# A graph-attention layer with residual and layernorm on one core: three edits in the prologue

## The reference, cut to what matters

```
dep_emb = dep_emb_table[adj]                                   # 64 wide
hi_t = h @ W1_w[:384] + dep_emb @ W1_w[384:] + W1_b
hj_t = h @ W2_w[:384] + dep_emb @ W2_w[384:] + W2_b
relevance = sum(hi_t * hj_t, axis=-1)                          # 64 x 64 for each graph
A = softmax(where(adj != 0, relevance, -1e9))
h_syn = relu((A @ h) @ gcn_w + gcn_b)
out = layernorm(x + h_syn @ Wo_w + Wo_b)
```

## Time and profile before

| | before |
|---|---|
| median of 3 runs | 372.6 us (372.27 to 373.13) |
| the profiled execution | 373.2 us |
| its span, first to last instruction | 371.3 us |
| PE busy | 364.5 us, 98% of the span |
| DVE busy | 274.7 us, 74% |
| ACT busy | 181.5 us, 49% |
| POOL busy | 145.1 us, 39% |
| PE's share of the chain that ended last | 95% |

### The profile page before, as it was taken

How to read it: one execution, slowest core, us unless ns; L and a number is a source line. 1 busy time by engine, 2 the same in 40 slices (tenths; PEclk the granted TensorE clock), 3 DMA queues, 4 the chain that set the end, 5 groups by cost and what they waited for, 6 DMA issues and landing times.

```text
span 371.3 us, 9946 instructions
## 1 busy us (share of the span) xinstructions
PE 364.5 (98%) x3827; PEld 316.8 (85%) x3827; DVE 274.7 (74%) x776; ACT 181.5 (49%) x374; POOL 145.1 (39%) x108
## 2 busy tenths in 40 slices
PE   8999999999999999999999999999999999999994
PEld 5688898988889898888989889898988989898894
DVE  1579778687786868788686777858677786877956
ACT  1576717164372715527272561816347181625574
POOL 1513551716134171513517152261714327141814
PEclk9999999999999999999999999999999999999998
DMA  7996014464443556354365524435553444550033
GB/s 221 352 327 200 24 29 170 158 187 156 139 145 96 173 169 184 116 158 162 89 182 169 179 94 155 160 118 184 169 160 108 129 159 149 171 171 4 2 127 132
DMA packets 43412, 55.48 MB, mean 149 GB/s; under 512 B 10368, under 2 KB 37632, under 8 KB 43392
## 3 DMA queue, kind: packets, MB, share of 16 engines
q1 hardware_dynamic: 42592, 54.44, 46.3%
q10 hardware_dynamic: 800, 0.77, 0.6%
HBM read 42.61 MB, written 12.58 MB: 149 GB/s over the span
## 4 chain that ended last, share of the span: by engine, by line
PE 95%; DMA 2%; DVE 1%; SPq 1%; ACT 0%; issue 0%; POOL 0%
PE banks L471 28%; PE banks L473 27%; PE banks L472 27%; PE banks L531 7%; PE banks L497 7%; DMA xt_sb<-in_x_t_dram 2%; DVE m_lo L920 0%; SPq L398 0%; ACT xt_hi L749 0%; PE banks L616 0%; DVE stats L871 0%; DVE xt_sb L866 0%; SPq L394 0%; POOL rstd L1239 0%; ACT xt_sb L832 0%
## 5 line engine op out<-in xcount | busy, mean ns | idle before, releaser
L1171 POOL TENSOR_TENSOR y_sb<-y_sb,wob_sb 128x1536 f32<-128x1536 f32 x15 | 52.8, 3522 | 88.0 <-DVE y_sb L888 73.9
L783 ACT CAST z_hi<-banks 128x512 fp32r<-128x512 f32 x48 | 26.6, 588 | 96.6 <-PE banks L531 90.8
L866 DVE TENSOR_TENSOR y_sb<-banks,y_sb 128x384 f32<-128x384 f32 x60 | 33.4, 556 | 47.3 <-PE banks L473 43.7
L472 PE MATMUL banks<-wo_lo,hs_hi 128*128 128x384 f32 x180 | 60.5, 336 | 0.0
L471 PE MATMUL banks<-wo_hi,hs_hi 128*128 128x384 f32 x180 | 60.5, 336 | 0.0
L473 PE MATMUL banks<-wo_hi,hs_lo 128*128 128x384 f32 x180 | 60.5, 336 | 0.0
L471 PE MATMUL banks<-z_hi,gcn_hi 128*128 128x512 f32 x144 | 58.3, 405 | 0.0
L471 PE MATMUL banks<-xt_hi,m_hi 128*128 128x512 f32 x144 | 57.1, 397 | 0.5 <-DVE u_sb L922 0.5
L473 PE MATMUL banks<-xt_hi,m_lo 128*128 128x512 f32 x144 | 56.5, 392 | 0.0
L473 PE MATMUL banks<-z_hi,gcn_lo 128*128 128x512 f32 x144 | 56.5, 392 | 0.0
L472 PE MATMUL banks<-z_lo,gcn_hi 128*128 128x512 f32 x144 | 56.1, 390 | 0.0
(11 more groups left out here) (108 smaller groups left out, 614.7 us busy)
## 6 DMA issues: line engine op xcount, KB each, us to landing
x_sb<-in_x_dram SPq DMA_DIRECT2D x16, 768.0 KB, 4.7
xt_sb<-in_x_t_dram SPq DMA_DIRECT2D x15, 768.0 KB, 6.4
y_sb<-in_x_dram SPq DMA_DIRECT2D x15, 768.0 KB, 4.5
out_dram<-y_sb SPq DMA_DIRECT2D x30, 384.0 KB, 2.5
adj_sb<-in_adj_dram SPq DMA_DIRECT2D x32, 64.0 KB, 3.0
xt_sb<-in_x_t_dram SPq DMA_DIRECT2D x2, 384.0 KB, 7.1
xt_sb<-in_x_dram SPq DMA_DIRECT2D x1, 768.0 KB, 6.2
w2t_sb<-in_w_t_dram SPq DMA_DIRECT2D x3, 192.0 KB, 4.6
```

The lines of the kernel that those rows point to most:

```text
L472: pe.matmul(acc, a_hi, b_lo, start=False, stop=False)
L783: act.copy(by_graph(z_hi[:, f, :]), mixed(f)).then_inc(zhi, 1)
L866: dve.tensor_tensor(y_home(g, slot)[:, q, :], out_bank(g, q)[:, 0:HID], y_home(g, slot)[:, q, :], ALU.add).then_inc(added, 1)
L1171: pool.tensor_tensor(y_home(g, slot), y_home(g, slot), wob_sb[:].rearrange("p (o n) -> p o n", o=1).to_broadcast([P, PAIRS, HID]), ALU.add ...
```

## The change

Four edits, all in the prologue.

- The c products and the waits ahead of them move from behind M's first round to between its second and third blocks.
- The u product, one plain fp32 product of `ones` and `u_diag`, becomes two fp32r products of `ones_r` (a rounded copy of `ones`) with `u_hi` and `u_lo`. VectorE makes `ones_r` by one more copy, `u_hi` by the three instructions that made `u_diag`, and `u_lo` by three more, each of which reads `ident` and `u_hi` and takes a column of `u_sb` as scalar.
- Rounding the second half of group 0's x^T moves from ScalarE (L749) to VectorE, between the low parts of the first half and those of M. GpSimd's low part of it waits for a new semaphore `xt0_half`.
- GpSimd's later `split_x` counts one fewer in `xhi`, since ScalarE no longer adds one for that half. VectorE also waits once for its own `ones`.

```diff
@@ TensorE
-            def m_stage(c):
+            def m_stage(c, blocks=range(C)):
                 pe.wait_ge(w12_loaded[c], 32)
-                for d in range(C):
+                for d in blocks:
...
             pe.wait_ge(zero_column, 1)
-            m_stage(0)
+            m_stage(0, range(C - 1))
...
             mm.then_inc(c_mm, 1)
+            m_stage(0, range(C - 1, C))
             pe.wait_ge(c2_ready, 2)
...
             pe.wait_ge(u_diag_ready, 1)
-            pe.matmul(U_BANK[:, 0:HID], ones[:].to_broadcast([P, P]), u_diag, start=True, stop=True).then_inc(u_mm, 1)
+            pe.matmul(U_BANK[:, 0:HID], ones_r[:].to_broadcast([P, P]), u_hi[:], start=True, stop=False)
+            pe.matmul(U_BANK[:, 0:HID], ones_r[:].to_broadcast([P, P]), u_lo[:], start=False, stop=True).then_inc(u_mm, 1)
@@ ScalarE
-            act.wait_ge(xt_loaded[0], 16)
-            act.copy(xt_hi[:, 0, :, GT // 2:GT], xt_sb[:, 0, :, GT // 2:GT]).then_inc(xhi, 1)
@@ VectorE
+            dve.wait_ge(xt_loaded[0], 16)
+            dve.tensor_copy(xt_hi[:, 0, :, GT // 2:GT], xt_sb[:, 0, :, GT // 2:GT]).then_inc(xt0_half, 1)
             for d in range(C):
                 dve.wait_ge(m_hi_ready, d + 1)
...
             dve.wait_ge(u_sb_ready, 1)
+            dve.tensor_copy(ones_r[:], ones[:])
             for d in range(C):
-                a = dve.tensor_scalar(u_diag[:, d * P:(d + 1) * P], ident[:], u_sb[:, d:d + 1], None, ALU.mult)
+                a = dve.tensor_scalar(u_hi[:, d * P:(d + 1) * P], ident[:], u_sb[:, d:d + 1], None, ALU.mult)
+            a.then_inc(u_hi_ready, 1)
+            dve.wait_ge(u_hi_ready, 1)
+            for d in range(C):
+                a = dve.scalar_tensor_tensor(u_lo[:, d * P:(d + 1) * P], ident[:], u_sb[:, d:d + 1],
+                                             f32(u_hi[:, d * P:(d + 1) * P]), ALU.mult, ALU.subtract)
             a.then_inc(u_diag_ready, 1)
@@ GpSimd
             def split_x(g, slot):
-                pool.wait_ge(xhi, g + 1)
+                pool.wait_ge(xhi, g)
...
-            pool.wait_ge(xhi, 1)
+            pool.wait_ge(xt0_half, 1)
             pool.tensor_tensor(xt_lo[:, 0, :, GT // 2:GT], xt_sb[:, 0, :, GT // 2:GT],
                                f32(xt_hi[:, 0, :, GT // 2:GT]), ALU.subtract).then_inc(xlo, 1)
```

More of the change, by code:

```diff
@@ L155, in gnn_layernorm_kernel @@
         ones = sb("ones", [P, 1])
+        ones_r = sb("ones_r", [P, 1], F32R)
         zero = sb("zero", [P, 1])
@@ L169, in gnn_layernorm_kernel @@
         u_sb = sb("u_sb", [P, C])
-        u_diag = onehot[:].rearrange("p m t -> p (m t)")[:, PAIRS * HID:(PAIRS + 1) * HID]
+        u_hi = sb("u_hi", [P, HID], F32R)
+        u_lo = sb("u_lo", [P, HID], F32R)
         products = onehot[:].rearrange("p m t -> p (m t)")[:, 0:PAIRS * HID].rearrange("p (q d) -> p q d", d=HID)
@@ L227, in gnn_layernorm_kernel @@
         xt0_hi = sem("xt0_hi")
+        xt0_half = sem("xt0_half")
         xt0_lo = sem("xt0_lo")
@@ L238, in gnn_layernorm_kernel @@
         u_sb_ready = sem("u_sb_ready")
+        u_hi_ready = sem("u_hi_ready")
         u_diag_ready = sem("u_diag_ready")
@@ L895, in _ @@
             dve.memset(ones[:], 1.0).then_inc(ones_ready, 1)
+            dve.wait_ge(ones_ready, 1)
             dve.memset(adj_max[:], 0).then_inc(max_zero, 1)
```

## The result

| | before | after |
|---|---|---|
| median | 372.75 us (4 runs) | 376.89 us (4 runs, 376.77 to 377.16) |
| profiled execution | 373.2 us | 376.88 us |
| its span | 371.3 us | 375.1 us |
| ratio | | 1.0107, 95% interval 1.0093 to 1.012 |

A forecast was written before the change was run, and what follows sets the result against it. TensorE's own list, once through the prologue, was taken to bound the kernel. A u product starting 2.48 us later, +0.07 after a pause, -0.32 for cheaper products, gave +2.2 on the 372.6 us median: 374.8 us, range 372.0 to 375.6.

The forecast's parts named there:

- want the same port at the same time: Prologue: GpSimd asks at 14.97 and gets the SBUF port before VectorE's third `u_lo`, due at 15.13.
- 2.7 us of standing still: Ahead of the u product: TensorE idle from about 16.2 to 18.9 us, waiting for `u_lo`.
- `u_lo` at 0.85 us for three: VectorE, prologue: three two-input instructions, taken as 0.85 us between bounds of 0.68 and 1.1.
- the u product's gain of 0.32: TensorE: two rounded products at 0.33 us replace one fp32 product at 0.65, saving 0.32 us.
- Forecast for this part: The u product: +2.48 us later start, +0.07 for a first product after a pause, -0.32 for cheaper products: +2.2 us.
- rival C: Behind the u product: the forecast's wait plus a lower clock costing 1.9 us more, 376.7 us; chance 0.06.
- The four things at 14.29: Projection's start: ScalarE's rounding, VectorE's `m_lo` and `u_sb`, GpSimd's low part, TensorE; first three called within 0.06 us.
- The edge block: M's first round: second edge block lands at 6.4 us, so TensorE idles 0.6 us before the c products at 6.5.
- VectorE's rounding of x^T's second half: Prologue: copy of 768 columns starting at 11.39, taken as 0.55 us between 0.53 and 0.95.
- GpSimd's start: Low part of group 1's x^T starts at 14.97, hanging on ScalarE's copy at 13.42 after data land at 13.35.
- rival B: Prologue: VectorE finishes all of `u_lo` before GpSimd starts, both gains stand, 372.0 or 371.9 us; chance 0.24.
- The gain at the start: Projection's start: moves from 14.29 to 14.05 us, a gain of 0.24 us.

The follow-up runs named there:

- pool_waits: Kernel after, with GpSimd's low part of group 1's x^T made to wait until `u_lo` is ready; 372.56 us, ratio 0.999.
- parts_1_2: Kernel after with `u_diag` and the single fp32 u product put back; 372.64 us, ratio 0.999.
- pool_waits_b: The same kernel as pool_waits, measured once more in another group; 372.71 us, ratio 0.9989.
- pause: Kernel before, with TensorE's u product also waiting for GpSimd's low part of group 1's x^T; 376.29 us, ratio 1.0092.
- part_3: Kernel before with only the u product split into two rounded ones; 377.05 us, ratio 1.0096.
- one_input: Kernel after, u's columns split first so that `u_hi` and `u_lo` are six `tensor_scalar` instructions with one SBUF input each; 376.72 us, ratio 1.009.
- warm_once: Kernel after with one fp32 product of zeros on TensorE ahead of the wait for `u_lo`; 376.55 us, ratio 1.0086.

## Why the prediction failed, step by step

**Right:** what bounds the kernel; that VectorE's `u_lo` and GpSimd's low part of group 1's x^T want the same port at the same time; that the loser waits out a whole instruction; 2.7 us of standing still (2.69 measured); `u_lo` at 0.85 us for three (0.88 undisturbed, in pool_waits); the u product's gain of 0.32 (0.30 between parts_1_2 and pool_waits, with 0.18 us between the two halves). Forecast for this part was +2.2 us; -0.52 + 2.86 - 0.20 makes +2.14. That the restart came out so close, 18.91 against 18.78, is partly luck: GpSimd ended 0.81 us earlier than forecast, but it then had the three `u_lo` still ahead of TensorE, 0.89 us, and not the last one's 0.15.

**Wrong, and the cause of the miss:** the clock, rival C. The sum has no term for it. The prediction said "a pause of this length just about does not bring it down here" and gave it 0.06. The mechanism and its price were on the page (1.9 us forecast, 1.58 measured, 376.7 against 376.89); the chance was wrong. I took the idle end of one profile, where the clock stayed full for at least 2.5 us, for a bound. That was one sample of something that varies: in the fourteen profiles of this case the time from TensorE's last product to the fall of the clock, at that same idle end, is 2.3 us (pool_waits_b) to 5.3 (parts_1_2), 3.2 in the kernel before, and a stop of 1.88 us was enough in `pause`. With a stop of 2.7 us the clock fell in all four executions of the kernel after and in four of six of part_3 and one_input, so C was the likely case, and the forecast should have been C's 376.7.

**Wrong without consequence:**

- The four things at 14.29. The three within 0.06 us of each other are `m_lo`, `u_sb` and GpSimd's low part; ScalarE, named first, was done with M at 13.37 and is not one of them.
- The edge block. I let it land at 6.4 us and had TensorE idle for 0.6 us. In the profile after it landed 3.7 us after its issue at 1.2, at 4.9, and there was no gap. TensorE was slower than I had it: its four records took 2.14 us in place of 4 x 0.345 = 1.38. So the c products started at 6.39, close to the 6.5 of the forecast, by luck and for another reason. Weight loads in that round lasted up to 333 ns against a median of 190, products up to 980 ns against 487, twice as long, though the granted clock reads 1.00 there, as it does for the first zero products (weight loads 337 ns). How far this reaches varies: in the kernel before only the first product shows it (591 ns), in part_3 the whole round took 3.21 us for six records.
- VectorE's rounding of x^T's second half. I had it at 0.55 us between bounds of 0.53 and 0.95; it took 0.69. It started at 10.58, before M's blocks were there, and held nothing up.
- GpSimd's start. I had it at 14.97, tied to a landing at 13.35; it was 14.37, since the data landed before 12.81, when ScalarE's copy began without waiting for them. `u_lo` came 0.15 us earlier than forecast and GpSimd 0.60, so all three pieces lost the port rather than the last. The 0.16 us on which rival B rested was smaller than what a landing moves between two executions.
- The gain at the start. The projection began 0.52 us earlier than in the earlier trace rows, yet pool_waits, where it starts at 13.62, is only 0.1 to 0.3 us faster in the median. In the profiled execution of the kernel before the second half of x^T landed at 11.39. `pause` has the same code up to that point, and there ScalarE rounded that half from 10.32, straight behind the first:

```profile
8.16 4.15 PE L571 MATMUL banks<-w2t_sb,w1t_sb 128*128 128x385 f32 x12
...
13.44 0.38 PE L608 MATMUL banks<-c_sb,ones 128*128 128x3 f32 x2
13.69 0.48 PE L471 MATMUL banks<-xt_hi,m_hi 128*128 128x512 f32 x1
```

The projection starts at 13.69 without any wait. So the 0.53 us wait that I had set out to see removed belongs to the execution that was profiled, not to every one.

## What to carry to other kernels

Before adding VectorE instructions that read and write SBUF, look for the long GpSimd instruction that will run beside them: the price isn't their length but what is left of GpSimd's, here 3.5 us for 0.9 us of work, and one wait that orders the two the other way cost nothing here, where GpSimd had slack. A stop of TensorE can cost half as much again through the clock (2.9 us of waiting, 1.6 behind it), also when TensorE is back at work before the clock falls; price it in, and don't take one profile in which the clock held for a bound. And a wait that ends with a DMA in a single profile may not exist in the median: take landings from several.

## What the runs showed of the hardware that I had not expected

- The clock fell only after the pause was over: 0.5 us after TensorE's restart in the profile after, 0.6 in `pause`, 1.1 in warm_once.
- It fell after pauses of 1.88 and 2.03 us and held through one of 1.38; between these no run here looks. With stops of 2.0 to 2.8 us (warm_once, part_3, one_input) it held in at least two executions of six each.
- A `tensor_scalar` with one SBUF input and a column as scalar waits for GpSimd like an instruction with two (3577 ns for 275).
- The row of the granted clock does not show the slow start: 1.00 where weight loads take 337 ns in place of 190.
